# A decoder layer on one core: 1/sqrt moved from POOL to ACT, and the prologue taken apart

## What is computed

```python
def _layernorm(x, axis=-1, eps=1e-05):
    return (x - mean(x)) / sqrt(var(x) + eps)
# attention: at each token, its 16 heads attend to one another
q = rope((x @ Wq.T + bq)); k = rope((x @ Wk.T + bk)); v = x @ Wv.T + bv
att = softmax(einsum('bshd,bstd->bsht', q, k) / sqrt(32.0))
x = _layernorm(x + einsum('bsht,bstd->bshd', att, v) @ Wo.T + bo)   # with heads and tokens swapped
# mLSTM: queries x, keys and values ctx; gates from both
D = exp(log_D - max_log_D)                     # 128x128 per head, lower triangle
C = einsum('bhsd,bhtd->bhst', qh, kh) / sqrt(32.0) * D
h = einsum('bhst,bhtd->bhsd', C / normalizer, vh)
hn = (h - mu) * rsqrt(var + EPS) * ln_scale    # per token and head
x = _layernorm(x + hn)
# experts: eight, a score each, the best one is applied
d = x - select_mean_diff;  score = sum((select_weight . d / norm(d)) ** 2)
gate = sigmoid(imp_slope * (score - imp_center)); best = argmax(gate)
x = _layernorm(x + (1 - gate[best]) * x + gate[best] * (bias_w[best] + degen[best] @ (upd[best] @ (x - debias_w[best]))))
```

## Time and profile before

| what | us |
|---|---|
| runs | 1709.47, 1708.28, 1704.01; median 1708.28 |
| the profiled execution's own time | 1706.93 |
| its span | 1705.2 |
| busy: PE / DVE / POOL / ACT | 1520.7 / 1283.2 / 955.2 / 855.4 |

### The profile page before, as it was taken

The page is one execution under the profiler, slowest core; times in us unless marked ns, Lnnn a source line. Parts: engine busy times, 40 slices in busy tenths (PEclk is TensorE's granted clock), DMA queues, the critical chain, the costliest instruction groups (busy, mean ns, idle before and its releaser), DMA issues.

```text
span 1705.2 us, 67667 instructions
## 1 busy us (share of the span) xinstructions
PE 1520.7 (89%) x27398; PEld 1196.0 (70%) x27398; DVE 1283.2 (75%) x3337; ACT 855.4 (50%) x2385; POOL 955.2 (56%) x1232
## 2 busy tenths in 40 slices
PE   0789999999999999999999999999999999999955
PEld 0667777777777777777777777777777777777743
DVE  4346777787787778777877787778778877877764
ACT  2035545545554555455545554555555455645551
POOL 1025556555655665566556655665565556556653
PEclk9899999999999999999999999999999999999985
DMA  4123333333433343333233333333343334333310
GB/s 155 38 84 106 105 105 101 108 105 99 123 103 106 99 123 98 112 99 122 96 104 109 118 99 95 120 108 105 96 123 105 105 99 123 102 108 99 105 58 31
DMA packets 195142, 174.71 MB, mean 102 GB/s; under 512 B 141887, under 2 KB 143551, under 8 KB 186890
## 3 DMA queue, kind: packets, MB, share of 16 engines
q1 hardware_dynamic: 195082, 173.87, 33.4%
HBM read 139.76 MB, written 34.08 MB: 102 GB/s over the span
## 4 chain that ended last, share of the span: by engine, by line
POOL 31%; PE 25%; DVE 21%; issue 19%; ACT 2%; SPq 1%; POOLq 1%; DMA 0%; DVEq 0%; ACTq 0%
POOL h_rs L777 12%; POOL Dx L762 5%; PE quad L418 5%; POOL rs L791 4%; POOL r L786 4%; DVE Dx L969 3%; PE bank L365 3%; PE bank L513 2%; PE bank L490 2%; PE bank L458 2%; PE bank L526 2%; POOL nm L814 2%; POOL c L770 2%; PE bank L373 2%; PE bank L374 2%
## 5 line engine op out<-in xcount | busy, mean ns | idle before, releaser
L757 POOL TENSOR_TENSOR ex<-ex,w_rec 128x512 f32<-128x512 f32 x64 | 67.2, 1050 | 543.7 <-DVE w_rec L910 543.7
L652 ACT ACTIVATE Dx<-Mb,a_col 128x128 f32<-128x128 f32 x1024 | 312.9, 395 | 7.6 <-DMA Mb<-m_rows 7.4
L777 POOL TENSOR_TENSOR h_rs<-h_ve,half_neg 128x16 f32<-128x16 f32 x64 | 207.1, 3236 | 8.5 <-DVE h_ve L987 1.7
L622 ACT ACTIVATE x1T<-bank 128x512 f32<-128x512 f32 x64 | 38.2, 597 | 314.4 <-PE bank L365 314.4
L762 POOL TENSOR_SCALAR_AFFINE_SELECT Dx<-Dx 128x512 f32<-128x512 f32 x256 | 159.9, 636 | 8.6 <-ACT Dx L652 8.6
L969 DVE SCALAR_TENSOR_TENSOR Dx<-quad,Dx 128x512 f32<-128x512 f32 x256 | 157.1, 668 | 7.3 <-PE quad L478 7.3
L946 DVE TENSOR_SCALAR x<-r,mv,rs 128x512 f32<-128x512 f32 x64 | 54.3, 849 | 129.6 <-POOL rs L791 129.6
L791 POOL TENSOR_TENSOR rs<-ve,half_neg 128x1 f32<-128x1 f32 x192 | 104.8, 546 | 37.7 <-DVE ve L931 37.6
L659 ACT ACTIVATE Hs<-quad 128x528 f32<-128x528 f32 x64 | 39.1, 611 | 171.3 <-PE quad L500 171.3
L478 PE MATMUL quad<-x1T,cT 32*128 32x128 f32 x2048 | 76.6, 286 | 43.3 <-issue 26.9
L373 PE MATMUL bank<-wq_high,x_high 128*128 128x512 f32 x256 | 115.1, 449 | 0.0
(11 more groups left out here) (163 smaller groups left out, 4357.4 us busy)
## 6 DMA issues: line engine op xcount, KB each, us to landing
Mb<-m_rows SPq DMA_DIRECT2D x64, 1024.0 KB, 4.6
xb<-in_x SPq DMA_DIRECT2D x256, 64.0 KB
xr<-in_x SPq DMA_DIRECT2D x64, 256.0 KB, 3.0
cb<-in_ctx SPq DMA_DIRECT2D x64, 256.0 KB, 2.6
v_rows<-v_sb SPq DMA_DIRECT2D x64, 256.0 KB, 3.3
VG<-v_rows SPq DMA_DIRECT2D x64, 256.0 KB, 3.9
out_dram<-yo SPq DMA_DIRECT2D x64, 256.0 KB, 3.1
Dx<-in_wq SPq DMA_DIRECT2D x4, 256.0 KB, 4.7
```

What stands on the lines that cost most here:

```text
L652: last = go(Dx[t.parity()][:, j, n, :], Mb[t.parity()][:, h, :], ACT.Exp, bias=a_col[t.parity()][:, h:h + 1], scale=-1.0)
L777: tt(h_rs[:], h_ve[:], half_neg[:], ALU.pow).then_inc(s.hrs_sb, 1)
```

## The change

The powers on POOL and their constant half_neg go. ACT computes exp(-0.5 ln(ve)) by two activations in a row, the second waiting for the first, at four places of its step: for layernorm 2 (`n_2(e)`) ahead of m_Hs, for the mLSTM's norm (`n_h(d)`) between the first and the second group of m_Dx, for layernorm 3 (`n_3(g)`) ahead of p_v's copy, and for layernorm 1 (`n_1(b)`) between x_yo and m_x1T. On POOL the mask of the group j=2 moves ahead of y2, and nm3 behind y2. m_QK no longer waits for masks. DVE's x1 waits explicitly for r2 of two tiles before.

In the prologue the weights get a semaphore each; SP loads x of tile 0, the identity and the biases, then wq, wv, wk, x of tile 1, wo, and the remaining eight constants last. ACT's and DVE's work on a weight stands inside step 0, in the order q, v, k, and TensorE's p_q, p_v, p_k each wait for their own. The low part of wo stays on POOL, under its own semaphore. The constants are waited for at the start of step 2. The experts' constants are multiplied at the end of DVE's step 1, and summed on TensorE at the start of step 3, into another bank. WARM is 68, and it waits only for the memsets.

```diff
 def p_q(t):                       # TensorE; p_v, p_k and a_proj likewise
-    if t.k == 0 and t.regs is None:
-        pe.wait_ge(s.low_set, 4)
+    if begins(t, 0):
+        pe.wait_ge(s.low_set, 1)
+        pe.wait_ge(s.bias_step, 5)
 def m_QK(t):
-    for j in range(3):
-        pe.wait_ge(s.Dm_sb[j], upto(t))
+def x_constants():                # TensorE, step 3
+    pe.wait_ge(s.prod_set, 3)
+    pe.wait_ge(s.KT_sb, 3)
+    for c in range(CH):
+        last = mm(bank[6][:, 0:NW], ones_f[:], wx_prod[:, c, :], start=(c == 0), stop=(c == CH - 1))
+    last.then_inc(s.shift_ps, 1)
-WARM = 62
+WARM = 68
...
+def rsqrt(t, ve, ln, rs, ve_sem, ln_sem, rs_sem, used):      # ACT
+    act.wait_ge(ve_sem, upto(t))
+    go(ln[:], ve[:], ACT.Ln).then_inc(ln_sem, 1)
+    act.wait_ge(ln_sem, upto(t))
+    edge(act, t, (used, 1))
+    go(rs[:], ln[:], ACT.Exp, scale=-0.5).then_inc(rs_sem, 1)
...
-def rsqrt(t, ve, rs, ve_sem, rs_sem, used):                  # POOL
-    pool.wait_ge(ve_sem, upto(t))
-    edge(pool, t, (used, 1))
-    tt(rs[:], ve[:], half_neg[:, 0:1], ALU.pow).then_inc(rs_sem, 1)
-def r_pow(t):
-    pool.wait_ge(s.hve_sb, upto(t))
-    edge(pool, t, (s.y1_sb, 1))
-    tt(h_rs[:], h_ve[:], half_neg[:], ALU.pow).then_inc(s.hrs_sb, 1)
...
 def a_x1(t):                                                 # DVE
     dve.wait_ge(s.rs1_sb, upto(t))
-    edge(dve, t, (s.r2_sb, 2), (s.x1T_ps, 2))
+    dve.wait_ge(s.r2_sb, upto(t, 2))
+    edge(dve, t, (s.x1T_ps, 2))
...
-dve.wait_ge(s.w_in, 16 * 4 * CH)
+def w_split(n, nth):          # DVE, step 0, for q, v, k: scale (q alone), split the bias, low part
+    dve.wait_ge(s.w_in[n], 16 * CH)
```

More of the change, by code:

```diff
@@ L265, in chunks, with begins @@
             return t[:].rearrange("p c n -> p (c n)")
+        def begins(t, k):
+            return t.regs is None and t.k == k
         def edge(eng, t, *pairs):
@@ L690, in x_yo, with n_1, n_h, n_2 @@
                 go(yo[:], y3[t.parity()][:], ACT.Identity, bias=nm3[:], scale=rs3[:]).then_inc(s.yo_sb, 1)
+            def rsqrt(t, ve, ln, rs, ve_sem, ln_sem, rs_sem, used):
[4 more added lines that the diff above has]
+                go(rs[:], ln[:], ACT.Exp, scale=-0.5).then_inc(rs_sem, 1)
+            def n_1(t):
+                rsqrt(t, ve1, ln1, rs1, s.ve1_sb, s.ln1_sb, s.rs1_sb, s.x1_sb)
+            def n_h(t):
+                rsqrt(t, h_ve, h_ln, h_rs, s.hve_sb, s.hln_sb, s.hrs_sb, s.y1_sb)
+            def n_2(t):
+                rsqrt(t, ve2, ln2, rs2, s.ve2_sb, s.ln2_sb, s.rs2_sb, s.x2_sb)
+            def n_3(t):
+                rsqrt(t, ve3, ln3, rs3, s.ve3_sb, s.ln3_sb, s.rs3_sb, s.yo_sb)
             nc.scalar.preload_act_table_set("natural_log_exp_and_others")
-            act.wait_ge(s.const_in, CONST_IN)
-            act.wait_ge(s.w_in, 16 * 4 * CH)
-            act.wait_ge(s.scale_set, 1)
-            for n in range(4):
+            def w_raise(n):
+                act.wait_ge(s.w_in[n], 16 * CH)
+                if n == 0:
+                    act.wait_ge(s.scale_set, 1)
                 for c in range(CH):
@@ L741, in step @@
                 if b.real():
+                    n_1(b)
                     m_x1T(b)
@@ L820, in _ @@
             last.then_inc(s.pads_set, 1)
+            pool.wait_ge(s.pads_set, PADS)
+            pool.wait_ge(s.high_set, 4)
+            for c in range(CH):
+                last = tt(w_low[3][:, c, :], w_in[3][c], w_high[3][:, c, :], ALU.subtract)
+            last.then_inc(s.lowo_set, 1)
+            pool.wait_ge(s.lowo_set, 1)
+            pool.wait_ge(s.const_in, CONST_IN)
             tt(wg_ctx[:], wg_sb[:, 1], wg_sb[:, 2], ALU.add).then_inc(s.mean_set, 1)
@@ L839, in step @@
                     m_mask(c, 1)
-                if b.real():
-                    rsqrt(b, ve1, rs1, s.ve1_sb, s.rs1_sb, s.x1_sb)
-                if c.real():
                     m_mask(c, 3)
@@ L846, in step @@
                     a_scale(a)
-                if d.real():
-                    rsqrt(d, ve2, rs2, s.ve2_sb, s.rs2_sb, s.x2_sb)
                 if e.real():
@@ L1122, in _ @@
[L1122 to L1130 removed]
+                dve.wait_ge(s.high_set, nth + 1)
                 for c in range(CH):
@@ L1133, in _, with x_products, x_constants @@
                 last.then_inc(s.low_set, 1)
+            def x_products():
+                dve.wait_ge(s.const_in, CONST_IN)
+                for c in range(CH):
+                    middle = wx_sb[:, c, 2 * nw:NW]
+                    tt(wx_prod[:, c, 0:nw].rearrange("p (n r) -> p n r", r=NR),
+                       wx_sb[:, c, 0:nw].rearrange("p (n r) -> p n r", r=NR),
+                       middle.unsqueeze(2).broadcast_to([P, NX, NR]), ALU.mult)
+                    last = tt(wx_prod[:, c, nw:2 * nw].rearrange("p (n r) -> p n r", r=NR),
+                              wx_sb[:, c, nw:2 * nw].rearrange("p (n r) -> p n r", r=NR),
+                              debias_sb[:, c, :].unsqueeze(2).broadcast_to([P, NX, NR]), ALU.mult)
+                last.then_inc(s.prod_set, 1)
+                tt(wx_prod[:, :, 2 * nw:NW], wx_sb[:, :, 2 * nw:NW], wx_sb[:, :, 2 * nw:NW],
+                   ALU.mult).then_inc(s.prod_set, 2)
+            def x_constants():
+                dve.wait_ge(s.shift_ps, 1)
+                nc.vector.tensor_copy(wx_shift[:], bank[6][:, 0:NW]).then_inc(s.shift_set, 1)
+                dve.wait_ge(s.shift_set, 1)
             def step(a):
@@ L1138, in step @@
                     p_low(a)
+                if begins(a, 0):
+                    for nth, n in enumerate((0, 2, 1)):
+                        w_split(n, nth)
+                if begins(a, 3):
+                    x_constants()
                 if c.real():
```

147 lines of the change are left out of this document (78 added, 69 removed).

## The result

| | before | changed |
|---|---|---|
| median (us) | 1708.88 | 1595.83 |
| range, 4 runs each | 1704.01 to 1717.51 | 1591.46 to 1599.87 |
| profiled span | 1705.2 | 1596.5 |
| first neg_max / last neg_max / end | 73.3 / 1624.4 / 1705.2 | 36.7 / 1516.0 / 1596.5 |

A forecast was written before the change was run, and what follows sets the result against it. TensorE was taken to bound the step, with 1.39 us of waiting to win. Span 1705.2 - 36 (start) - 46.5 (steps) - 3 (end) + 1 (constant's matmuls) = 1620.7, plus 1.7: 1622.4, stated as 1623; range 1603 to 1652.

The forecast's parts named there:

- The start: Prologue: weights loaded first bring KT of tile 0 near 32.6 us and first neg_max near 37; 36 us won.
- a doubling: Prologue, p_k on TensorE: at the slow clock its 3.5 us would double, total 1626 instead of 1623.
- The step's mechanism: Steady step: QK no longer waits for masks, x starts earlier behind rs1; 0.75 us less per step, -46.5 us in all.
- the spare: Steady step, rs1's arrival: 0.5 us of spare, beyond which each further 0.1 us late costs 0.1 per step.
- The rival of swapped tables: ACT in the step: Ln and Exp need tables swapped, some 6.3 us a step, about 2058 us; chance 0.01.
- only its 1.39 us of waiting can be won: Steady step on TensorE: busy 23.15 of 24.54 us, so at most 1.39 us of idle time can go.
- -0.62 for QK: TensorE before the QK matmuls: the 0.62 us wait for POOL's masks goes.
- -0.17 for x1T: TensorE before the x1T transposes: the 0.17 us wait for DVE's x goes.
- -0.18 for the scores: TensorE before the next score matmuls: half of the 0.36 us wait for DVE's four products Dx goes.
- +0.2 for Y: TensorE before Y: ACT's copy Hs starts later, behind the pair for rs2, adding 0.2 us.
- the gapless rival: Steady step: TensorE never waits, 1.2 us a step won, 1595 us; chance 0.11.
- The end: Last steps: TensorE no longer waits up to 6.93 us for masks; 3 us off, 1 to 5.

The follow-up runs named there:

- the last version: Kernel with rs2's pair behind the copies and H inside q, plus a_col and eFM on ACT moved directly behind cT: 1575.23 us, ratio 0.9223.

## Why the prediction fell short

**The start** was right: first neg_max at 36.7 for "near 37". KT starts almost where the sum put it, at 32.98 for 32.6, but two misses of that sum nearly cancel, which is luck. The low half of k's weight was ready at 28.16 for 29.1, since DVE began 0.65 us earlier and its chain was shorter by the rest; and k's product then took 4.73 us for 3.5:

```profile
25.66 2.50 DVE L1161 TENSOR_TENSOR wk_low<-Dx,wk_high 128x512 fp32r<-128x512 f32 x4
```

```profile
28.21 0.39 PE L382 MATMUL bank<-bias,ones_bf 128*128 128x512 bf16 x1 [1.98 <-DVE wk_low L1161]
```

```profile
32.98 1.05 DVE L920 STREAM_TRANSPOSE KT<-bank 128x512 f32<-128x512 f32 x1 [4.20 <-PE bank L389]
```

What was weighed against it came in part. TensorE had no work for 1.98 us ahead of k. From 28 to 32 us, while k's product runs, the granted clock (third from the right) is 0.57, so mostly the lower level, 1.2 of 2.4 GHz:

```profile
28.00:32.00 4.00, 3.79 (x10) 2.99 (x11) 0.79 (x2) 0.94 (x2) 2.90 (x3) 0.57 0.63 204
```

k takes 4.73 us from its bias (28.21) to its end (32.94), against 3.20 in the steady step (805.67 to 808.87). That is 1.5 us, not the 3.5 of a doubling, since from 31.7 to 33.0 us the granted clock is 0.89, mostly the full 2.4 GHz again; KT was 0.4 late in all. The Trainium skill's rule (TensorE: Matmul & The Clock Gate, section "Part 1: The HAM clock gate"), that the clock falls when TensorE idles and returns under sustained work, agrees with this trace for k too.

**The step's mechanism** was right, and the runs bear it out point by point: no wait before QK, x behind rs1, and the mask wait worthless by itself (with x early it costs 0.23 us a step). Of the spare the prediction said 0.5 us and the trace has 0.46. The rival of swapped tables fell, with one load in the whole run:

```profile
L738 ACT ACT_TABLE_LOAD  x1: 1283/1283/1283, 0.8 to 0.8; - x1
```

**The step that failed** is the bound in the first paragraph, "only its 1.39 us of waiting can be won", and with it the sum "-0.62 -0.17 -0.18 +0.2 = -0.77". Both took the idle entry as the price of a wait. Its terms, with what they measured:

- -0.62 for QK: -0.665. -0.17 for x1T: -0.240. Each wait took its overlap with it.
- -0.18 for the scores, half of 0.36 "since some issue time stays": the whole entry went, in the mean 0.253, and with the overlap it was -0.320. I sized it on one step, whose 0.36 was above the mean, and halved it without a row that showed such issue time; what the loop's turn does cost stood at x's transposes.
- +0.2 for Y: +0.117. Hs started at 796.45, ahead of the second activation's end at 796.54; the forecast had named that overlap and not counted it.
- Not forecast: -0.077 between L's and x's transposes, where the loop's turn came out of the way once KT was early.

Together -1.185 instead of -0.77. Of the 0.415 us between, 0.20 are the overlap of the three waits, 0.08 the loop's turn, 0.08 the smaller price of Hs, and 0.07 the halved wait, less 0.02 for QK's entry. A period 1.21 us shorter is what the gapless rival had, with a chance of 0.11, and it hit the number by luck: its argument against itself, "Y's wait cannot vanish", was right, and Y's 0.28 stayed. With that wait still there the step fell to what a gapless TensorE seemed to need because the true floor lies lower: at 22.99 us the last version has won 1.53 us, more than the 1.39 that there were to win.

The Trainium skill describes such an overlap (TensorE: Matmul & The Clock Gate, section "Part 2: What happens when you issue a matmul"): the drain of one matmul, 128 cycles, lies under the fill of the next; an estimate from this at 2.4 GHz is 53 ns. The runs have 61 to 70 ns, at six places (the three above, Y's, the masks' wait put back, and the scores' wait with rs1 late); that it is the drain that comes into view there no run shows.

**The end** was right in its mechanism, 4.2 us of waiting for "1 to 5", and wrong in its result: the clock, which the prediction looked at only for the start, took back 3.9.

## What to carry to other kernels

Price a wait on a pipelined engine from start to start, not by its idle entry: here each was worth 0.06 to 0.07 us more, and a floor taken from busy time was too high by that much per wait. Before removing the largest wait ask what stands one group behind it: the 0.60 us before QK were worth nothing until x came earlier. After an edit that adds or removes instructions in a loop, compare the instruction queue's packets before blaming the edit: with the mask wait back, 16 instructions of shift made over 100 us (1727 to 1767 against 1610 to 1622).

## What the runs showed of the hardware that was not expected

A loop's jump back on TensorE can take 3.8 to 5.3 us instead of 0.21, with nine packets of the instruction queue at each such turn, 141 and 159 packets per run instead of 42, and up to 10 us more in one step. That these packets are TensorE's own code fits all fourteen traces, but no row names it. Which places are bad, and why the stalls are frequent in one kernel and rare in the next, the runs don't settle. The changed kernel lies 16 instructions from such a place; the medians of its neighbours with more warm-up were 17 and 39 us higher, of which the one stall in each trace explains 9 and 11.

In the last 80 us the granted clock was 0.67, 0.59 and 0.74 for the same 415 useful matmuls. Over the twelve traces without filling the kernels that waited less there got the lower clock (0.58 to 0.63 against 0.62 to 0.71) and ended no sooner beyond the scatter; with matmuls without use in the waits the clock was the highest of all.
